# Weighted sums of a quad of heads in two bursts, and other steps for the casts and remainders of the splits

## What is computed

```python
raw = jnp.einsum('bhid,bhjd->bhij', q, k)
scores = sips_alpha[0] * jnp.tanh(raw / sips_beta[0])
soft_bits = jnp.tanh(x @ hex_w.T)
scores = scores + lam * jnp.einsum('bid,bjd->bij', soft_bits, soft_bits)[:, None] / 2.0
hexc = jnp.tanh(x @ q6_w.T)
lat = jnp.einsum('bid,hde,bje->bhij', hexc, Mh, hexc) / 6.0
scores = scores + lat * (jax.nn.sigmoid(scale_logit) * 2.0)
attn = jax.nn.softmax(jnp.where(causal, scores, -jnp.inf), axis=-1)
x = _layernorm(x + einsum('bhij,bhjd->bhid', attn, v).reshape(b, t, D) @ out_w.T)
r = jax.nn.sigmoid(xr @ W_r.T); k_act = jnp.square(jax.nn.relu(xk @ W_k.T))
x = _layernorm(x + r * (k_act @ W_v.T))      # xr, xk: mixes of x and the position before
```

## Time and profile before

| | us |
|---|---|
| three runs, median (lowest to highest) | 420.8 (420.11 to 423.27) |
| profiled execution, its own time | 420.74 |
| its span from first to last instruction | 418.8 |
| busy in the span: TensorE | 368.2 (88%) |
| VectorE | 332.7 (79%) |
| ScalarE | 327.3 (78%) |
| GpSimd | 230.6 (55%) |
| mean granted clock of TensorE, of full speed | 0.985 |
| tanh of pair 0 in batches 1, 3, 4, 6 and 7 starts at | 85.72, 174.38, 219.24, 308.04, 350.06 |

### The profile page before, as it was taken

One profiled execution on the slowest core, in us unless ns is written; L12 is line 12 of the kernel. 1 busy time (PEld: TensorE's weight loads), 2 busy tenths in 40 slices (PEclk: granted clock), 3 DMA queues, 4 the chain that ended last, 5 costly groups with the idle time before them and its releaser, 6 DMA issues.

```text
span 418.8 us, 8760 instructions
## 1 busy us (share of the span) xinstructions
PE 368.2 (88%) x2907; PEld 191.3 (46%) x2907; DVE 332.7 (79%) x539; ACT 327.3 (78%) x364; POOL 230.6 (55%) x367
## 2 busy tenths in 40 slices
PE   4557798899999999999899989999989998999863
PEld 1232343345455544645364535454544554345442
DVE  4873677988988989798979897989887958786643
ACT  1002389999998989799889989899989998999621
POOL 4313535834687359644965488646873446344532
PEclk9999999999999999999999999999999999899978
DMA  3354587786621775167624764276318610100000
GB/s 100 94 144 121 162 275 189 232 236 166 200 84 48 205 193 172 49 164 195 190 80 121 188 182 131 85 194 186 123 52 206 173 59 7 45 27 1 2 27 25
DMA packets 37807, 53.74 MB, mean 128 GB/s; under 512 B 3522, under 2 KB 35266, under 8 KB 36190
## 3 DMA queue, kind: packets, MB, share of 16 engines
q1 hardware_dynamic: 34078, 51.49, 43.4%
q10 hardware_dynamic: 3696, 1.84, 1.8%
HBM read 38.69 MB, written 14.61 MB: 127 GB/s over the span
## 4 chain that ended last, share of the span: by engine, by line
PE 50%; DVE 15%; issue 10%; POOL 9%; SPq 7%; ACT 5%; DMA 3%; ACTq 1%; POOLq 0%; DVEq 0%
PE raw L511 22%; PE side_bank L511 13%; PE sums L511 12%; DVE probs L1004 6%; ACT probs L788 3%; PE side_bank L598 3%; POOL probs L892 2%; SPq L401 2%; ACT probs L783 2%; POOL x L927 2%; POOL x L923 2%; SPq L415 2%; POOL parts L905 2%; SPq L412 2%; DVE bn L1089 1%
## 5 line engine op out<-in xcount | busy, mean ns | idle before, releaser
L1004 DVE SCALAR_TENSOR_TENSOR probs<-probs,scal,raw 128x1024 f32<-128x1024 f32 x160 | 202.8, 1274 | 40.4 <-PE raw L511 39.4
L783 ACT ACTIVATE probs<-raw 128x1024 f32<-128x1024 f32 x160 | 163.9, 1025 | 33.2 <-PE raw L511 32.2
L892 POOL TENSOR_SCALAR_AFFINE_SELECT probs<-probs 128x256 f32<-128x256 f32 (+1 forms) x224 | 98.9, 458 | 131.6 <-ACT probs L788 131.1
L788 ACT ACTIVATE probs<-probs 128x1024 f32<-128x1024 f32 x160 | 169.3, 1060 | 0.9 <-DVE probs L1004 0.9
L511 PE MATMUL raw<-q_stack,k_stack 72*128 72x384 bf16 (+3 forms) x512 | 99.0, 306 | 10.9 <-DVE probs L1004 6.9
L511 PE MATMUL raw<-i_stack,j_stack 111*128 111x384 bf16 (+3 forms) x512 | 98.1, 304 | 2.7 <-ACT probs L783 2.5
L511 PE MATMUL sums<-probs,values 128*32 128x256 f32 (+2 forms) x1280 | 93.3, 391 | 5.1 <-POOL probs L892 4.1
L511 PEld LDWEIGHTS raw<-q_stack,k_stack 72*128 72x128 bf16 x512 | 38.9, 99 | 63.8 <-DVE probs L1004 35.3
L511 PEld LDWEIGHTS raw<-i_stack,j_stack 111*128 111x128 bf16 x512 | 42.4, 99 | 48.6 <-issue 15.3
L511 PEld LDWEIGHTS sums<-probs,values 128*32 128x32 f32 x1280 | 29.8, 109 | 50.9 <-issue 27.2
L899 POOL TENSOR_TENSOR whole<-whole,parts 128x512 f32<-128x512 f32 x22 | 26.2, 1189 | 23.1 <-DVE parts L1038 23.1
...
...
## 6 DMA issues: line engine op xcount, KB each, us to landing
...
```

Of the source, the lines that this page charges most:

```text
L783: nc.scalar.activation(pair_probs(t), raw[:, t % PSUM_PAIRS, :].rearrange("p (u i) -> p u i", u=2), ACT.Tanh).then_inc(tanh_done, 1)
L788: nc.scalar.activation(pair_probs(t), pair_probs(t), ACT.Exp).then_inc(exp_done, 1)
L892: last = nc.gpsimd.affine_select(out=v, in_=v, compare_op=ALU.is_ge, fill=0.0, base=0, pattern=[[0, v.shape[1]], [1, P]], channel_multipli ...
L1004: v.scalar_tensor_tensor(out=o, in0=o, scalar=scal[:, 2:3], in1=raw[:, t % PSUM_PAIRS, :].rearrange("p (u i) -> p u i", u=2), op0=ALU.mult ...
```

## The change

The weighted sums of a quad come in two bursts instead of five parts: the first multiplies block 0 of the four heads with 512 columns at a time, the second blocks 1, 3 and 2 (384, 128 and 256 columns). They stand in steps 6 and 9, 11 and 14, 16 and 19, 21 and 24 (1 and 4 of the next batch). The first waits for the masks of the quad's pairs 0 and 1, the second for the mask of pair 4. `pv_done` rises by 2 and by 3. `values_in` and v1 move from step 7 to step 11, y and the residual from 10 to 9, kk from 16 to 15, `inv_std` from 10 to 11, in one step with `norm`. Of the casts, hi Q moves from step 5 to 4, hi K from 9 to 5, hi J from 11 to 7, mid Q from 9 to 8, mid K from 11 to 10, mid J from 15 to 12, mid G from 17 to 16; hi G stays in 13. Of GpSimd's subtractions, rest Q moves from 6 to 5, rest K from 10 to 6, rest J from 13 to 8, lo J from 16 to 14; lo Q (10), lo K (13), rest G (14) and lo G (17) stay. `sums_out` stays in steps 5 and 15.

```diff
-VALUES_STEPS = [6, 7, 7, 9, 11, 11, 12, 13, 14, 15, 16, 18, 19, 19, 19, 20, 20, 24, 25, 25]
+VALUES_STEPS = [(6, 9), (11, 14), (16, 19), (21, 24)]
-VALUES_UNITS = {7: ["v1"]}
+VALUES_UNITS = {11: ["v1"]}
...
-            def weighted(b, par, t):
+            def weighted(b, par, quad, part):
...
-                pe.wait_ge(mask_done, PAIRS * b + last_of_group(t) + 1)
+                first_pair = PAIRS_PER_QUAD * quad
+                pairs = (2, 3)[part]
+
+                pe.wait_ge(mask_done, PAIRS * b + first_pair + (2 if part == 0 else PAIRS_PER_QUAD))
...
+                blocks = [[(0, lambda r: head(r // 2, r % 2, 0, T))],
+                          [(1, lambda r: head(2 + r // 2, r % 2, 0, 3 * P)),
+                           (3, lambda r: head(2 + r // 2, r % 2, 3 * P, T)),
+                           (2, lambda r: head(4, r // 2, (r % 2) * 2 * P, (r % 2 + 1) * 2 * P))]][part]
+                for jb, cols_of in blocks:
+                    for r in range(4):
+                        last = mm(sums[32 * r:32 * r + 32, jb * P:T], values[par][:, jb, 4 * quad + r, :], cols_of(r),
+                                  start=(s == 0 and part == 0), stop=(s == 1 and jb == 2), skip_group_check=True)
+                last.then_inc(pv_done, pairs)
...
-            PREP = {6: [(rest, Q)], 10: [(lo, Q), (rest, K)], 13: [(lo, K), (rest, J)], 14: [(rest, G)],
-                    16: [(lo, J)], 17: [(lo, G)]}
-            POST = {10: [(inv_std, 0)], 11: [(norm, 0)], 18: [(gated_residual,)], 19: [(inv_std, 1), (norm, 1)]}
+            PREP = {5: [(rest, Q)], 6: [(rest, K)], 8: [(rest, J)], 10: [(lo, Q)], 13: [(lo, K)],
+                    14: [(lo, J), (rest, G)], 17: [(lo, G)]}
+            POST = {11: [(inv_std, 0), (norm, 0)], 18: [(gated_residual,)], 19: [(inv_std, 1), (norm, 1)]}
```

40 lines of the change are left out of this document (14 added, 26 removed).

## The result

The changed kernel takes 445.6 us (median of four, 439.21 to 446.13), the kernel before 420.46 beside it (four, 418.96 to 423.27): 1.051 times as long, 95% interval 1.044 to 1.057. That is 25 us more, where 7.7 were forecast, and outside the range of 420 to 437. The profiled execution took 445.62, its span is 443.7, and the mean granted clock of TensorE in it is 0.929 instead of 0.985.

What follows compares the result with a forecast made beforehand. No engine is full; how their orders fit sets the time. Full batches 5 x (0.3 + 0.5) = 4.0, batch 0 0.6, batches 6 and 7 2.2, end 0.9: 7.7 us more, 428 us, range 420 to 437.

Steps and rivals of the forecast that it cites:

- the mechanism of the border: At a batch's start, 512 columns moved ahead of scores(2) make the tanh of pair 2 0.5 us later.
- the second half with kk: Later steps of a batch, kk one step earlier and 768 columns in step 19 as before: no gain or loss.
- the chain of 9.1 over the norm: Steps 11 to 15: exp(8), mask, inv_std and norm, x1T, mask(9), 768 columns, scores(15) put T(15) 9.1 us behind T(11).
- the tail waits for the last mask: At the kernel's end the whole 768 columns wait for the last mask, where 256 did: +0.9 us, nothing hides it.
- Step 0 and 1: 512 columns cost nothing in step 0, where scores(1) waited for main(19); moved to step 1 they cost +0.5 us.
- batches 6 and 7: The last two batches have no casts to relieve, so the wait at T(15) grows: +1.1 us each, 2.2 together.
- Step 6: 512 columns instead of 256 ahead of scores(7): +0.44 us on TensorE, taken as +0.3.
- Casts: mid J, hi G and hi K may wait for running GpSimd operations: 0 to 2.4 us a batch, taken as +0.5.
- Steps 9 to 15: Step 9 gains 0.65, step 11 loses about 1.0; norm then sets T(15), leaving +0.3 us a full batch.
- Batch 0: The first batch has no post work; v1 and 512 columns in step 11 cost it 0.6 us.
- The rows go out no later: DMAs same in number, lo Q, lo K, lo G in the same steps, lo J two earlier: cost at nothing.
- A: Rival: hi K, mid J and hi G all caught by GpSimd, delaying y and kk, 436 us; chance 0.22.

Runs made afterwards that it cites:

- before21: The kernel before with only the bursts of pairs 15 and 16 (512 columns) moved from step 0 to step 1 of the next batch: 425.8 us, ratio 1.011.
- b20v7: burst20 with v1 and its copy back in step 7: 439.7 us, 1.040 times the kernel before.
- filler: The changed kernel with the transposes of xT2 in step 0 made three times: 440.9 us, 1.044 times the kernel before.
- b20loq9: burst20 with GpSimd's lo Q in step 9 instead of 10: 428.9 us, 1.014 times the kernel before.
- burst20: The changed kernel with the first burst of quad 3 in step 20 (step 0 of the next batch) instead of 21: 434.3 us, 1.030 times the kernel before.
- b20p7: burst20 with the first burst of quad 0 in step 7 instead of 6: 431.6 us, 1.021 times the kernel before.
- b20inv10: burst20 with inv_std back in GpSimd's step 10, norm staying in 11: 432.5 us, 1.023 times the kernel before.
- combo7: burst20 with the edits of b20loq9, b20p7 and b20inv10 together: 431.3 us, 1.017 times the kernel before.
- combo8: combo7 with the first burst of quad 0 in step 8 instead of 7: 428.6 us, 1.012 times the kernel before.
- combo9: burst20 with the edit of b20p7, and GpSimd's lo Q and then rest J both in step 9: 430.0 us, 1.018 times the kernel before.

## Why the prediction was wrong

**Right.** The side (slower), that TensorE's busy time falls by about 1 a batch while the batch is longer (0.8 and 1.6), the mechanism of the border (+0.5; 0.6 at T(2) in before21), that the second half with kk is even, that casts are caught by GpSimd's operations, the chain of 9.1 over the norm (9.2 in b20v7), and that the tail waits for the last mask.

**Step 0 and 1, the first step that failed.** "They cost nothing there" was right of the scores and wrong of TensorE. The 512 columns were the engine's work while it waited for main(19). Without them it has nothing for 0.94 to 2.20 us, at three of seven borders its clock goes down for some 3 or 7 us, and T(2) came 2.6 to 3.6 later there, in batches 3, 5 and 6, where +0.5 was forecast. The profile of before had the signs: 0.38 of wait behind 1.07 of work. The clock stood in no term of the sum. It cost some 4.7 in batches 1 to 5 (filler), and it goes with most of what batches 6 and 7 have above the forecast: 2.7 at T(2) of batch 6, and in batch 7 T(14) to T(15) is 5.8 instead of 2.1. b20loq9, whose x1T waits as long in batch 7 (1.16) at full clock, takes 3.6 there, so some 2.2 of the 5.8 go with the clock and 1.5 with the order.

**Step 6** was under-sized: 0.8 between T(6) and T(7) (burst20 against before; b20p7 takes it away) instead of 0.3.

**Casts.** The mechanism was right, the list was not. mid K in step 10, against lo Q, was left out although both stand in one step. It costs 0.9 in three of five batches and 0.2 in the others (b20loq9); 0.5 a batch was taken for all casts together. What made it dear is the work behind: main(10), then the copy of the values, which the change had put into step 11 right ahead of G2. hi K, on the list, was free in four of the five full batches of after, and caught in batches 1 and 3 of burst20 (1.37). The count of one caught cast before was low as well: in the batch shown hi K (0.63), hi G (0.53) and mid J (1.22) all end 0.28 behind a GpSimd operation.

**Steps 9 to 15.** The forecast let the norm set T(15). In the full batches TensorE's own order did, with G2 behind the copy of the values; b20inv10 left T(15) where it was. In batch 2 T(11) came 1.3 later than before where +0.15 to +0.5 was forecast, and T(15) 9.8 behind it where 9.1 was.

**Batch 0** is 2.7 longer instead of 0.6, and why stays open. "The rows go out no later" left out a wait at its other end: hi Q overwrites `parts` and must wait until the rows written from it are out. In batch 0 of after:

```profile
58.93 0.43 DVE L1036 CAST parts<-whole 128x512 bf16<-128x512 f32 x1 [3.03 <-DMA q_rows<-parts]
...
60.61 0.61 PE L511 MATMUL raw<-q_stack,k_stack 72*128 72x384 bf16 x4 [2.59 <-DVE probs L1002]
```

Before, this wait was 0.49 long. main(5) stands behind the cast, the scores behind main, and the clock is low from 62.9 to 69.7. But the move of hi Q from step 5 to step 4 is not shown to be the cause. b20loq9, with hi Q in step 4, waited 1.43 and its batch 0 took 45.1, as before; before21, with hi Q in step 5 and nothing of batch 0 changed, waited 2.76 and took 46.3. The wait runs from 0.49 to 4.61 over the kernels, and hi Q was moved back alone in none.

**Of the rivals** A came nearest (collisions, 436), with the wrong casts. None had the clock.

**Open.** What decides whether a wait costs the clock: in after 1.52 did (batch 5) and 2.20 (batch 7) did not, behind y 1.28 did in combo7 and 1.36 did not in combo8, and executions of one kernel differ. The 4.5 that combo9 still loses in batch 7 and the tail was read (T(14) to T(15) 3.6 instead of 2.1, the last burst 2.15 instead of 0.64), not tested by an edit.
